# Conv block with 3x3 local attention: the q projection as three fp32r products into the score banks, all of V ahead of it, scores behind the tenth conv unit

## The reference

```python
perceived = conv3x3_depthwise(x, w_perc) + b_perc        # 128 -> 384 channels
hid = gelu(w_up1 @ perceived + b_up1)                    # 384 -> 256
h   = x + (w_up2 @ hid + b_up2)                          # 256 -> 128
q, k, v = split(h @ w_qkv.T + b_qkv)                     # per pixel
scores[i] = (q * shift(k, pos_i)).sum(-1) / sqrt(128)    # the 9 neighbours
out = h + sum_i softmax(scores)[i] * shift(v, pos_i)
```

## Time and profile before

| | |
|---|---|
| median of 3 runs | 412.9 us (412.62 to 414.03) |
| the profiled execution | 412.48 us, its span 410.7 us |
| mean granted TensorE clock | 0.989 |
| PE busy | 386.6 us, 94% |
| PEld busy | 353.2 us, 86% |
| DVE busy | 317.5 us, 77% |
| ACT busy | 306.1 us, 75% |
| POOL busy | 183.3 us, 45% |

### The profile page before, as it was taken

One profiled execution on the slowest core, in us unless ns is written; L12 is line 12 of the kernel. 1 busy time (PEld: TensorE's weight loads), 2 busy tenths in 40 slices (PEclk: granted clock), 3 DMA queues, 4 the chain that ended last, 5 costly groups with the idle time before them and its releaser, 6 DMA issues.

```text
span 410.7 us, 10251 instructions
## 1 busy us (share of the span) xinstructions
PE 386.6 (94%) x3618; PEld 353.2 (86%) x3618; DVE 317.5 (77%) x886; ACT 306.1 (75%) x681; POOL 183.3 (45%) x158
## 2 busy tenths in 40 slices
PE   2798898999999999999999999999999999999794
PEld 1698697898989999898989999898989989898484
DVE  4987868686878868686887868686897868784866
ACT  6533488877886987778786987778786987876782
POOL 6928663544434363544435364453435354230100
PEclk9979999999999999999999999999999999999998
DMA  8320020305031040404022040404022030301003
GB/s 251 139 65 1 19 100 0 117 2 168 2 116 52 18 152 0 166 0 165 1 85 81 9 157 0 166 0 165 1 70 96 0 102 2 104 15 40 0 25 131
DMA packets 11369, 28.57 MB, mean 70 GB/s; under 512 B 2385, under 2 KB 3025, under 8 KB 11345
## 3 DMA queue, kind: packets, MB, share of 16 engines
q1 hardware_dynamic: 10496, 28.20, 20.1%
q10 hardware_dynamic: 848, 0.05, 0.1%
HBM read 19.86 MB, written 8.39 MB: 69 GB/s over the span
## 4 chain that ended last, share of the span: by engine, by line
PE 78%; DVE 8%; ACT 3%; issue 2%; POOL 0%; DVEq 0%; ACTq 0%
PE m_ps L440 41%; PE s_ps L512 9%; PE work L450 9%; PE work L476 7%; PE work L471 7%; PE s_ps L495 5%; DVE t L799 2%; ACT p_sb L697 1%; DVE y L884 1%; DVE y L889 1%; DVE h_around L1016 1%; DVE ps_sb L873 1%; DVE y L887 1%; ACT m L619 1%; DVE ru_sb L874 0%
## 5 line engine op out<-in xcount | busy, mean ns | idle before, releaser
L440 PE MATMUL m_ps<-thi,whi 128*128 128x248 f32 (+1 forms) x576 | 171.1, 297 | 4.6 <-DVE wlo L812 2.7
L440 PE MATMUL m_ps<-thi,wlo 128*128 128x248 f32 (+1 forms) x576 | 161.7, 281 | 0.0
L440 PE MATMUL m_ps<-tlo,whi 128*128 128x248 f32 (+1 forms) x576 | 160.4, 278 | 0.0
L440 PEld LDWEIGHTS m_ps<-thi,whi 128*128 128x128 f32 x576 | 109.5, 190 | 11.6 <-issue 7.2
L440 PEld LDWEIGHTS m_ps<-tlo,whi 128*128 128x128 f32 x576 | 110.3, 191 | 4.2 <-issue 3.6
L440 PEld LDWEIGHTS m_ps<-thi,wlo 128*128 128x128 f32 x576 | 109.4, 190 | 0.0
L1106 POOL TENSOR_TENSOR hid_lo<-hid,hid_hi 128x1024 fp32r<-128x1024 f32 x30 | 71.9, 2396 | 20.8 <-ACT hid_hi L639 20.8
L683 ACT COPY pt<-ptc 32x256 f32<-32x256 f32 (+3 forms) x189 | 74.3, 393 | 5.8 <-DVE ptc L950 1.3
L629 ACT ACTIVATE hid<-y,b1eff 128x1024 f32<-128x1024 f32 x31 | 35.7, 1151 | 46.0 <-DVE y L897 25.5
L697 ACT ACTIVATE p_sb<-p_sb,negmax 128x101 f32<-128x101 f32 x128 | 47.0, 371 | 18.8 <-DVE negmax L931 18.8
L1113 POOL TENSOR_TENSOR p_sb<-p_sb,rsum 128x384 f32<-128x384 f32 x32 | 27.8, 870 | 68.0 <-DVE rsum L939 68.0
(11 more groups left out here) (124 smaller groups left out, 714.9 us busy)
## 6 DMA issues: line engine op xcount, KB each, us to landing
xp<-x_planes SPq DMA_DIRECT2D x16, 640.0 KB, 5.2
xr<-x_rows SPq DMA_DIRECT2D x16, 512.0 KB, 4.1
out<-o_sb SPq DMA_DIRECT2D x28, 256.0 KB, 4.1
out<-y SPq DMA_DIRECT2D x4, 256.0 KB, 2.1
w1T<-w SPq DMA_DIRECT2D x1, 384.0 KB, 3.1
w2T<-w SPq DMA_DIRECT2D x1, 128.0 KB, 4.3
wqk_in<-w_qk SPq DMA_DIRECT2D x1, 128.0 KB, 4.3
mask_bf<-masks SPq DMA_DIRECT2D x1, 126.2 KB, 4.2
```

Source lines behind the costliest of these rows:

```text
L440: last = pe.matmul(m_ps[:, b, col + first:col + end], a[:, j, dy, half * P:(half + 1) * P], c[:, par, T_PLACE[j], first + by:end + by], st ...
```

## The change

Four edits that belong together.

1. q is no longer one fp32 product with `wqk` but the sum of three fp32r products: high half of the weights with high half of h, low weights with high h, high weights with low h. The halves of h are made anew for each image: ACT casts (`high_h`), DVE subtracts (`low_h`), each for two halves of 512 columns. The halves of the weights are made once at the start.
2. q is written to the banks `s_ps`, in which the scores are written later, instead of `work`. The last image keeps the old form.
3. All three V parts now stand together before unit 8, and q behind unit 8.
4. The scores stand behind unit 9.

```diff
@@ tensor
+            def project_q_parts(n, c):
+                if from_image(n, 2):
+                    pe.wait_ge(rmax_done, n * 8 + (4 * c - 12))
+                if from_image(n, 3):
+                    pe.wait_ge(o_done, n * 2 + (c - 5))
+                cols = slice(c * CH, (c + 1) * CH)
+                pe.wait_ge(h_hi_done, n * 2 + (c - 1))
+                pe.matmul(s_ps[:, c, :], wqk_hi[:, :], h_hi[:, cols], start=True, stop=False)
+                pe.matmul(s_ps[:, c, :], wqk_lo[:, :], h_hi[:, cols], start=False, stop=False)
+                pe.wait_ge(h_lo_done, n * 2 + (c - 1))
+                pe.matmul(s_ps[:, c, :], wqk_hi[:, :], h_lo[:, cols], start=False, stop=True).then_inc(q_ready, 1)
...
+                    pe.wait_ge(wa_lo_done, 1)
...
-                    project_v(n, 1 - par, 0)
-                    project_q(n, 1 - par, 0, 2)
-                    project_q(n, 1 - par, 1, 0)
+                    for part in range(3):
+                        project_v(n, 1 - par, part)
                 units(8)
                 if attn:
-                    pe.wait_ge(q_done, n * 2 - 1)
-                    project_v(n, 1 - par, 1)
-                    pe.wait_ge(q_done, n * 2)
-                    project_v(n, 1 - par, 2)
-                    scores(n, 1 - par)
-                units(9, 10, 11)
+                    for c in range(NCH):
+                        project_q_parts(n, c)
+                units(9)
+                if attn:
+                    for g in range(2):
+                        pe.wait_ge(q_done, n * 2 + (g - 1))
+                        score(n, 1 - par, g)
+                units(10, 11)
@@ scalar
+            nc.scalar.mul(wqk_hi[:, :], wa[:, C:2 * C], SCALE).then_inc(wa_hi_done, 1)
...
+            def high_h(n, hp, c):
+                act.wait_ge(h_done, n * 2 + (c - 1))
+                if from_image(n, 2):
+                    act.wait_ge(q_ready, n * 2 - 2)
+                nc.scalar.copy(h_hi[:, c * CH:(c + 1) * CH],
+                               h_of(n - 1, hp)[:, W + c * CH:W + (c + 1) * CH]).then_inc(h_hi_done, 1)
...
-                nc.scalar.activation(q_sb[:, c * CH:(c + 1) * CH], work[:, 2 if c == 0 else 0, :],
+                sums = work[:, 2 if c == 0 else 0, :] if is_last(n) else s_ps[:, c, :]
+                nc.scalar.activation(q_sb[:, c * CH:(c + 1) * CH], sums,
...
                 if more:
                     high_t(n + 1, 1 - par)
+                if attn:
+                    for c in range(NCH):
+                        high_h(n, 1 - par, c)
                 if conv:
                     gelu(n, 0)
@@ vector
+            def low_h(n, hp):
+                for c in range(NCH):
+                    cols = slice(c * CH, (c + 1) * CH)
+                    dve.wait_ge(h_hi_done, n * 2 + (c - 1))
+                    if from_image(n, 2):
+                        dve.wait_ge(q_ready, n * 2 - 2)
+                    nc.vector.tensor_tensor(h_lo[:, cols], h_of(n - 1, hp)[:, W + c * CH:W + (c + 1) * CH],
+                                            h_hi[:, cols].bitcast(F32), ALU.subtract).then_inc(h_lo_done, 1)
...
+            nc.vector.tensor_tensor(wqk_lo[:, :], wqk[:, :], wqk_hi[:, :].bitcast(F32), ALU.subtract).then_inc(wa_lo_done, 1)
...
                 if conv:
                     finish_y(n, 0)
+                if attn:
+                    low_h(n, 1 - par)
                 if more and from_image(n, 2):
                     low_t(n + 1, 1 - par)
```

More of the change, by code:

```diff
@@ L146, in build @@
         w2lo = sb("w2lo", [P, 2 * C], F32R)
+        h_hi = sb("h_hi", [P, PIX], F32R)
+        h_lo = sb("h_lo", [P, PIX], F32R)
+        wqk_hi = sb("wqk_hi", [P, C], F32R)
+        wqk_lo = sb("wqk_lo", [P, C], F32R)
         h_around = sb("h_around", [P, 2, W + PIX + W])
@@ L257, in build @@
         hlo_done = sem("hlo_done")
+        h_hi_done = sem("h_hi_done")
+        h_lo_done = sem("h_lo_done")
         w2hi_done = sem("w2hi_done")
+        wa_hi_done = sem("wa_hi_done")
+        wa_lo_done = sem("wa_lo_done")
         w2lo_done = sem("w2lo_done")
@@ L478, in project_v @@
                 last.then_inc(v_ready, 1)
[L480 to L488, removed]
             def score(n, hp, g):
@@ L859, in _ @@
             dve.wait_ge(consts_done, 2)
+            dve.wait_ge(wt_copied, 3)
+            dve.wait_ge(wa_hi_done, 1)
+            nc.vector.tensor_tensor(wqk_lo[:, :], wqk[:, :], wqk_hi[:, :].bitcast(F32), ALU.subtract).then_inc(wa_lo_done, 1)
             nc.vector.tensor_tensor(b1eff[:, :], work[:, 2, 0:2], b1[:, :], ALU.add).then_inc(b1_done, 1)
```

## The result

| | before | changed |
|---|---|---|
| median | 412.76 us (412.18 to 414.03) | 421.95 us (421.55 to 422.03) |
| profiled execution | 412.48 us, span 410.7 | 421.97 us, span 420.2 |

The ratio is 1.0216, 95% interval 1.0192 to 1.0241: slower, by 9.2 us at the medians. 420.0 was predicted, 415.0 to 424.0 as the range.

What follows compares the result with a forecast made beforehand. PE sets the pace at 23.22 us per image, with chains A and B only 0.34 shorter; chain B grows, so +0.73, +5.8 and +0.75 give +7.3 us, 420.0 predicted, 415.0 to 424.0 for 8 in 10.

Steps and rivals of the forecast that it cites:

- The balance of 0.34 us: Per image of the loop: chain A plus chain B is 22.88 us, against PE's 23.22 us.
- PE saves 0.34 per image: q on PE: six fp32r matmuls take 1.37 us instead of 1.71; PE alone would need 22.88 per image.
- Chain B: From V's start over q (start Q) and four exps to the next m13 copy: 8.91 us instead of 8.18.
- Chain A: From the start of ACT's m13 copy of half 1 over h to V's start: fixed length, 14.70 us.
- Unit 0 waits 0.54, V 0.08: PE's two waits per image: unit 0 for the m13 copy 0.54 us, V for h 0.08 us.
- The period: One image of the loop: 23.68 us against 23.22, between 23.61 from both chains and 23.72 with a restart loss at V.
- The sum: Whole execution: +0.73, +5.8 and +0.75, together +7.3 us on the profiled 412.48; 420.0 predicted for the median.
- Added work hidden: Casts on ACT and subtractions on DVE fit into free time, 1.4 and 1.9 us spare; POOL keeps 0.4.
- PE's saving comes through: Rival: unit 0's copy is there at Q+6.06, so the time falls by 5.1 us to 407.8; chance 8%.
- A partial wait: Rival: exps start 0.3 to 0.5 us earlier than worked out, period 23.0 to 23.5, 410 to 415.5 us; chance 6%.
- POOL or DVE late: Rival: subtractions delay tlo, POOL and DVE's transpose; 424 to 434 us; 8% for above 424, shared with q no cheaper.
- q no cheaper: Rival: fp32r products into the score banks cost up to the old 1.71 us, 425 us; within the 8% above 424.

Runs made afterwards that it cites:

- the early copy: Changed kernel with ACT's m13 copy of half 1 behind two exps instead of four: 422.97 us median, ratio 1.0248 to the kernel before.
- The second traces: One more traced execution each of the kernel before, the changed one and the one with q ahead of unit 8: spans 413.0, 419.6 and 406.5 us.
- q ahead of unit 8: Changed kernel with one move on PE: all V, then q, then unit 8, then the scores. 409.49 us median, ratio 0.9918 to the kernel before.

## Why the prediction was right

*The balance of 0.34 us.* Right. With B shortened, the period falls to PE's own 22.90 (22.88 was worked out); with it lengthened it follows the chains.

*PE saves 0.34 per image.* Right: q takes 1.37 in the changed trace. By the Trainium skill, page "TensorE: Matmul & The Clock Gate", section "Back-to-back issue gap", N/2.4 + 2.5 gives 216 ns for a warm matmul of 512 columns. Six would take 1.29 by that, an estimate; the trace has 229 ns each in both kernels, so the measured 1.37 decides, and the formula is 6% low for these products.

*Chain B.* Predicted V to the next copy 8.91; measured 248.52-239.53 = 8.99. The terms: q 2.94 behind V (2.92), take_q 243.36 = Q+0.89, table load at Q+3.21 (3.22), first exp at Q+4.58 (4.52). The last differs because the scores started at Q+2.50, not Q+2.41: unit 9 to scores took 1.13 instead of 1.04, so the way over DVE's maxima, not ACT's, was the later one by a hair. In the loop's other body the chain is 9.06.

*Chain A.* Predicted 14.70 from copy to V, measured 239.53-224.83 = 14.70.

*Unit 0 waits 0.54, V 0.08.* Measured 0.48 on average and, in the loop, none that the trace shows: in the image above DVE ends h at 239.48 and PE reaches V at 239.53. Unit 0 started 0.71 after the copy's start, where the prediction had 0.61 from the hand-over of 0.05 seen at V; from there PE needed 13.99 to V, 13.90 and 0.09 of restart. 0.71+13.99 = 14.70, so both routes arrive together and no second wait is left. That the chain over h stands right behind the wait of unit 0 is what the early copy shows.

*The period.* Predicted 23.68; measured over 13 images 381.87-97.14 for twelve and 97.14-73.50 for the first, together 308.37 or 23.72 each. The prediction had 23.61 from its two chains and chose 23.68 for a part of a restart at V. No such restart is in the loop; what filled the place is chain B, 8.99 and 9.06 in turn instead of 8.91. To that extent the near hit of the period is luck.

*The sum.* In the middle stretch I predicted +0.73 +5.8 +0.75 = 7.3; measured 7.7. The terms one by one: image 1 to 2 73.50-50.04 = 23.46, +0.70; images 2 to 15 +6.3; V of image 15 to its copy 8.85, +0.71. The profiled execution was another 1.8 later, 0.46 in the start and 1.34 in the end. The prediction put these at nothing, with up to 0.5 for the start. The second traces have differences of that size at all three kernels, but the medians too leave about 1.5 us outside the middle, as worked out above, and what costs them is open. The forecast of 420.0 was 2 us low: 1.5 for start and end, 0.4 for the middle, and 0.2 because the sum itself (412.9 and 7.3) gives 420.2, less 0.1 because the kernel before came out at 412.76.

*Added work hidden.* Right: POOL had 0.36 to spare where 0.4 was worked out, and q ahead of unit 8 runs the same work at PE's pace. DVE's idle time before the constant keys fell from 3.21 to 2.10, as the prediction said it would.

*The rivals.* "PE's saving comes through" failed at the point named for it: the copy is not there when unit 0 asks. It comes true once q stands one unit earlier and the scores with it. "A partial wait", "POOL or DVE late" and "q no cheaper" did not occur: the period was 23.72, POOL had its 0.36, and q took 1.37.

## What to carry to other kernels

When one engine is busy all the time, its work is worth its full price only down to the length of the loop through the other engines; measure that loop first, as distances between hand-overs (here copy to V and V to copy), not as busy shares. Moving an operation later on the busy engine costs nothing there, but lengthens the loop by the shift less the idle time that the loop had behind it: here q stands 2.27 later behind V and V to the copy grew by 0.81, since 1.21 of idle time before the exp and 0.34 of q's own time went. A wait that is taken away and comes back elsewhere at the same size points to a second limit of equal length, so look for what both have in common and shorten that.

## What the runs showed that I had not expected

The granted clock at the end. In the last image PE is idle for 2.5 us ahead of the second half of `up` (L527 before). Behind that stretch the clock stayed at 1.00 for all of PE's remaining work in one trace of the kernel before, and was 0.50 (1.2 of 2.4 GHz) for about 3 us in the other. That other one, columns as in the earlier trace rows, with the granted clock third from the end:

```profile
388.00:390.00 2.00, 0.66 (x1) 0.50 (x2) 1.31 (x4) 1.40 (x3) 0.00 (x0) 0.76 0.00 0
390.00:392.00 2.00, 2.00 (x3) 0.67 (x2) 0.46 (x1) 1.90 (x5) 0.00 (x0) 0.50 0.00 0
392.00:394.00 2.00, 2.00 (x9) 1.02 (x8) 1.34 (x4) 0.67 (x3) 0.00 (x0) 0.89 0.00 0
```

Each of the three kernels traced twice has one trace with the fall and one without, and the end is 1.1 to 1.3 us longer with it. What decides it was not tried.

The start. V of image 1 lies between 49.58 and 50.84 us over all ten traces, and differs between two traces of one kernel as well. In the changed kernel's two traces DVE's first t, beside a POOL operation, is not what separates them: it took 2.29 us in the first (L828, from 11.54) and 2.28 in the second, with V at 50.04 and 50.72. What does go with the spread, in all ten, is the granted clock. In the four traces with V at 50.7 to 50.8 it first falls to 0.50 between 20 and 21 us; in the six with V at 49.6 to 50.0 it falls before 19.6. Whether that is the cause was not tried.
